# Four fewer filler matmuls, an earlier key mask, and a product kept in PSUM, in a four-layer image kernel

## The reference

```python
x = x + window_attention(_gn(x))      # 7 x 7 windows, shifted by 3, 8 heads of 8 channels, softmax
x = x + _L1_conv_ref(_gn(x))          # signs of x (*) signs of the kernel, times Ka, plus bias
x = x + _L2_conv_ref(_gn(x))          # 3 x 3 convolution with the sign of its kernel
x = x + _L3_conv_ref(_gn(x))          # expand, 4-tap convolution along the tokens, silu gates, contract
```

```python
beta = mean(|xp|, channels)                                   # xp: x padded by 1
K = reduce_window(beta, add, 3 x 3) / 9
Ka = K * mean(|kernel|, (0, 1, 2))
return conv(sign(xp), sign(kernel)) * Ka + bias
```

## Time and profile before

| what | value |
|---|---|
| median of 3 runs | 222.25 us |
| the runs | 222.25, 220.94, 222.32 us |
| the profiled execution's own time | 222.39 us |
| its span, first to last instruction | 220.5 us |
| its mean granted TensorE clock | 0.992 |

### The profile page before, as it was taken

How to read it: one execution, slowest core, us unless ns; L and a number is a source line. 1 busy time by engine, 2 the same in 40 slices (tenths; PEclk the granted TensorE clock), 3 DMA queues, 4 the chain that set the end, 5 groups by cost and what they waited for, 6 DMA issues and landing times.

```text
span 220.5 us, 6793 instructions
## 1 busy us (share of the span) xinstructions
PE 206.8 (94%) x2734; PEld 144.1 (65%) x2735; DVE 158.5 (72%) x316; ACT 138.9 (63%) x294; POOL 95.4 (43%) x108
## 2 busy tenths in 40 slices
PE   7888999999999999999999999689799999899994
PEld 2456788888878778888787765444456665445441
DVE  4665699976978778868789739699997763616533
ACT  2438697778886898769877452168345363966631
POOL 0349999871124397241970158187324311000000
PEclk9999999999999999999999999799999999999999
DMA  6960000000000000000000000000165710001023
GB/s 210 443 263 0 3 3 6 0 4 3 3 3 3 3 4 0 3 3 4 3 3 0 4 3 0 3 20 22 42 135 126 178 23 0 0 3 73 0 106 113
DMA packets 4701, 10.03 MB, mean 45 GB/s; under 512 B 704, under 2 KB 3520, under 8 KB 4544
## 3 DMA queue, kind: packets, MB, share of 16 engines
q1 hardware_dynamic: 4528, 9.27, 13.3%
q10 hardware_dynamic: 144, 0.34, 0.4%
HBM read 5.03 MB, written 1.61 MB: 30 GB/s over the span
## 4 chain that ended last, share of the span: by engine, by line
PE 73%; DVE 12%; ACT 6%; issue 4%; DMA 2%; POOL 1%; SPq 1%; ACTq 0%; DVEq 0%; POOLq 0%
PE turned L707 12%; PE outs L727 10%; PE scores L696 10%; PE scores L915 5%; PE scores L916 4%; PE qkv L667 4%; PE qkv L677 4%; PE turned L943 3%; PE scores L824 3%; DVE x L1156 3%; PE scores L637 2%; PE outs L749 2%; DMA p<-parts 2%; PE scores L933 2%; PE turned L860 2%
## 5 line engine op out<-in xcount | busy, mean ns | idle before, releaser
L1036 DVE TENSOR_REDUCE mx<-scores 113x16 f32<-113x784 f32 x32 | 30.9, 965 | 9.5 <-PE scores L696 9.3
L707 PE MATMUL turned<-cst,d 113*113 113x113 f32 x256 | 33.3, 273 | 0.9 <-DVE d L1041 0.9
L707 PEld LDWEIGHTS turned<-cst,d 113*113 113x113 f32 x256 | 27.8, 178 | 8.5 <-issue 7.1
L476 ACT ACTIVATE pt<-turned 113x392 f32<-113x392 f32 x64 | 28.4, 495 | 7.1 <-PE turned L707 5.8
L1041 DVE TENSOR_TENSOR d<-scores,mx 113x784 f32<-113x784 f32 x32 | 31.2, 976 | 1.1
L208 POOL TENSOR_TENSOR kex<-ks,cst 128x784 f32<-128x784 f32 (+1 forms) x16 | 23.2, 1451 | 18.7 <-ACT ks L455 18.5
L288 POOL TENSOR_TENSOR rstd<-ve,mhalf 128x1 f32<-128x1 f32 (+1 forms) x15 | 8.7, 578 | 51.8 <-DVE ve L1002 51.7
L727 PEld LDWEIGHTS outs<-vsb,pt 113*49 113x49 f32 x1024 | 26.1, 125 | 6.1 <-issue 2.9
L446 ACT ACTIVATE scores<-rel 113x784 f32<-113x784 f32 x32 | 26.2, 818 | 5.0 <-PE scores L637 3.9
L727 PE MATMUL outs<-vsb,pt 113*49 113x18 f32 x1024 | 29.2, 199 | 0.0
L696 PE MATMUL scores<-kex,qs 32*49 32x196 f32 x512 | 28.2, 332 | 0.0
(11 more groups left out here) (121 smaller groups left out, 370.7 us busy)
## 6 DMA issues: line engine op xcount, KB each, us to landing
p<-parts SPq DMA_DIRECT2D x20, 112.5 KB, 2.2
x<-x_in SPq DMA_DIRECT2D x1, 1568.0 KB, 9.8
out<-res SPq DMA_DIRECT2D x8, 196.0 KB, 1.9
xw<-xw_in SPq DMA_DIRECT2D x2, 392.0 KB, 4.8
xw<-xw_in SPq DMA_DIRECT2D x1, 784.0 KB, 6.7
p<-parts SPq DMA_DIRECT2D x6, 108.8 KB, 3.0
ker<-ker_in SPq DMA_DIRECT2D x2, 288.0 KB, 10.1
late<-late_in SPq DMA_DIRECT2D x1, 417.0 KB, 10.7
```

Of the source, the lines that this page charges most:

```text
L476: act.activation(pt[0:WK, k % 2, j].rearrange("p n (w t) -> p n w t", w=2), ps_t[j][0:WK, :].rearrange("p (n w t) -> p n w t", n=4, w=2)[: ...
L707: mm = pe.transpose(ps_t[j][0:WK, n * P:n * P + WK], d[0:WK, k % 2, h:h + 2, :].rearrange("p a b -> p (a b)")[:, 0:WK], ident[0:WK, 0:WK])
L1036: dve.tensor_reduce(top, sc, AXX, ALU.max).then_inc(max_done, 1)
```

## The change

Three edits. The four fillers are taken out between `proj_v(0)` and `scores(0)` (2 stay of 6). On DVE, the mask of windows 0 and 1 now stands ahead of the moments of group 1. In `finish1` the product is written back into the PSUM bank that it was read from, and the second instruction reads it there; the SBUF tensor `prod` is gone.

```diff
-        prod = sb("prod", [P, 2, HALF])
@@ PE
             proj_v(0)
-            filler(ps_t[1], 6)
+            filler(ps_t[1], 2)
             pe.wait_ge(init_dve, 2)
             scores(0)
@@ DVE, start
+            dve.wait_ge(ks_ready, 1)
+            mask_keys(dve, 0, 0, 2).then_inc(kex_first, 1)
             dve.wait_ge(ld_x1, 16)
             window_moments(1).then_inc(gn_stats, 1)
-            dve.wait_ge(ks_ready, 1)
-            mask_keys(dve, 0, 0, 2).then_inc(kex_first, 1)
@@ DVE, finish1
-                dve.tensor_tensor(prod[:, i], bk[u % 4][:, 0:HALF], ka[:, i], ALU.mult).then_inc(prod_done, 1)
+                ps = bk[u % 4][:, 0:HALF]
+                dve.tensor_tensor(ps, ps, ka[:, i], ALU.mult).then_inc(prod_done, 1)
                 dve.wait_ge(prod_done, u + 1)
-                dve.scalar_tensor_tensor(out=xx, in0=prod[:, i], scalar=ww("b1"), in1=xx, op0=ALU.add,
+                dve.scalar_tensor_tensor(out=xx, in0=ps, scalar=ww("b1"), in1=xx, op0=ALU.add,
                                          op1=ALU.add).then_inc(x_done, 1)
```

## The result

The changed kernel took 219.4 us (median of 4 runs: 217.16, 218.76, 220.04, 220.09), the kernel before 221.79 us beside it (220.94 to 222.32, 4 runs): ratio 0.9898, 95% interval 0.9852 to 0.9945. That is faster by 1.0%, inside the forecast range and 1.5 us above the forecast 217.9.

What follows compares the result with a forecast made beforehand. PE was taken as the bound, with 73% of the chain that ended last. Span 220.5 - 0.93 - 0 - 2.1 - 1.3 = 216.2; with 1.9 outside the span, less 0.14, 217.9 us; range 216.4 to 220.5.

Steps and rivals of the forecast that it cites:

- Part 1: At the start, four of PE's six fillers ahead of the first scores go: gain 0.93 us.
- for PE both are early enough: At the start, whichever of DVE and POOL masks first, DVE's mask (near 11.4 or 12.23) does not hold PE.
- Part 2: At the start, DVE's mask moves ahead of the moments: costs 0 to 0.08 us, taken as 0.
- the cover to the hundredth: At the start, two fillers would end at 12.29, just behind DVE's mask at 12.23 in the old order.
- Part 3: In the first convolution, the product in PSUM frees L1156 from waiting for POOL: 2.1 us, bounds 0.87 and 4.2.
- The slot between the two box sums: In the first convolution, `third_part(dve, 0)` gets in between POOL's L331 and L333, with some 0.6 us to spare.
- Part 4: At PE's gap ahead of `mix` (138 to 140 us), a shorter wait avoids the half clock behind it: 1.3 us.
- rival 1: The half clock stays or turns up elsewhere: 219.2 us; chance 0.25 with the clock's part of rival 5.
- rival 5: Less PE work before 13 us drops the clock near 15 us, costing some 1.3 us; chance counted within rival 1's 0.25.
- rival 2: In the convolution, a missed slot or late ACT copies wait the gain away: 220.4, or 219.1 with the clock's; chance 0.12.
- rival 3: In `finish1`, L1156 is long for another reason and stays 1.36 us, only the fillers count: 221.3 us; chance 0.08.
- rival 4: In `finish1`, DVE reads and writes one PSUM bank in turns, 0.41 us more per product: 223.6 us; chance 0.05.

Runs made afterwards that it cites:

- the kernel with the mask last: The changed kernel without its two fillers ahead of the first scores, DVE's mask back behind the moments: 218.42 us, ratio 0.9873 to the kernel before.

## Why the prediction was right, and where it failed

The forecast was 217.9 us and the result 219.4: right in its sign and its range, with a fall of 2.4 us where 4.3 were forecast. Step by step:

- **Part 1** said 0.93 us. Measured alone 0.74 in the trace, 0.81 in the time at full clock. The step that failed is "for PE both are early enough" (said in part 2) and the cover to the hundredth: I compared ends with starts, and left out that the scores start a quarter of a microsecond after the mask's end (12.00 and 12.25 here, 11.85 and 12.11 in the kernel with the mask last). With the mask first the stretch is 0.53 us instead of 1.40, which is 0.87.
- **Part 2** said that the move alone gains nothing measurable. True beside six fillers (0.02 us). With two it gives 0.13 us (0.66 to 0.53), and with none 0.6. DVE did come first, by 0.1 us.
- **Part 3** said 2.1 us up to POOL's `third_part(1)`, of which 0.87 in group 0 and 1.23 behind it. Measured there, at full clock: 2.10, with 0.86 and 1.24. That is not luck, since the steps between hold one by one in the full-clock traces: 1.30 us are gained by `remainder(0)`, two `nmr` give 0.2 each, the box sum at L333 costs 0.4, and the `mix` gives 0.75 (0.7 forecast). The slot between the two box sums was found as described: 1.36 us for the third part (about 1.4 forecast). The path behind `third_part(1)` was taken as dense, and it was not. From there to the end of the span it is 60.6 to 61.0 us in the three full-clock traces with groups 1 to 3 in SBUF, and 59.7 to 60.4 in the seven with them in PSUM; by the times it is 0.5 us, 2.58 in all. The product's surcharge for writing PSUM, bounded by 0 and 0.41, is 0.006 us. Of the Trainium skill's 62 cycles more for a PSUM source ("VectorE: DVE Perf Modes", section "The TRN2 errata — SBUF-src ops pay a fixed extra latency per instruction"), the trace shows nothing: the addition takes 626 ns with a PSUM source and 627 undisturbed with an SBUF one.

  The chain that ended last in the fillers-only kernel (start, duration, what), ahead of `conv2(3)`:

```profile
170.90 0.60 SPq L262
171.54 0.60 SPq L262
172.19 1.79 SPq L262
174.02 2.30 DMA p<-parts
176.46 0.70 PE scores L838 x6
```

  SP's queue issues its DMAs back to back there, and PE waits for the last (0.27 us idle). With the product in PSUM these transfers start earlier, and the chain of the changed kernel's undisturbed run has no DMA behind `conv2(1)`. That this is all of the 0.5 us isn't shown: the kernel with no fillers and the mask first has the product in PSUM and such a wait too (0.30 us).

- **Part 4 is the step that failed.** It said that the half clock goes with the gap, for 1.3 us. The first half of it is shown: filling that gap alone brought 12 of 12 runs to full clock, and with group 0 in PSUM, which leaves 0.97 us of its 1.82, 11 of 12. But rival 1 came true as well. It spoke of a new wait of PE for box sums of about 1.7 us; the trace of before had this wait already, 1.51 us long, and the change made it 2.12. The clock fell behind it in two traces, and with it filled six of six runs stayed up. The change swapped one place for another. The early half clock of the profiled run, worth 1.7 us, was not foreseen: rival 5 looked for a fall near 15 us, this one came at 7 us, ahead of the edit in PE's list.
- The size in part 4 was off too. It took the 1.3 us between 220.94 and 222.25 for the price of the half clock, but 220.94 lies above all 24 full-clock runs, of which the slowest took 220.87. From 222.25 to full clock it is 1.8 us. So the base was the slower level, and the changed kernel's full-clock runs, at 217.33, lie below the forecast.
- At full clock the changed kernel takes 217.33 us against 220.44, 3.1 us less, and the sum without the clock was 3.0. That these agree so well is in part luck: the start gave 0.06 less than forecast and the end more, and the parts measured alone add up to 3.4 (0.81 + 2.58), or 3.5 with the mask's 0.13. The 0.3 to 0.4 us between the parts and the whole are not explained. In the traces they lie behind `third_part(1)`, where the changed kernel's undisturbed run waits 0.40 us for a DMA ahead of `conv2(1)` and the product-only run doesn't wait.
- What of the 219.4 is the change? Its ten runs have a median of 218.38, the kernel before 221.2 in most groups. The four first runs held both of the doubly disturbed ones. With the mean clock known for each run the two effects can be told apart; with medians of four they can't.
- **Rivals 2, 3 and 4** fall: the slot was not missed, L1156 lost its delay to the nanosecond, and the product in PSUM costs 6 ns. Rival 5, a clock fall by the removal of fillers, has no support: 4 of 12 at full clock without them, 24 of 68 with them.

## What to carry to other kernels

Follow a change along the waits to a named point, and check it there in a run at the same clock: that sum held to a hundredth, while the kernel's time moved by 3 us for another reason. When VectorE reads two SBUF tensors beside GpSimd, look at the spread of one line's durations; moving one input to PSUM removed it here. And when a chain beside PE gets faster, look for the waits of PE that it makes longer, not only for the one that it mends, since the clock may fall there as it did in the old one. Filler matmuls into a free bank, ended before the wait does, delayed `third_part(1)` by 0.03 us in the traces of both kernels that had them.

## What was unexpected of the hardware

- DVE read and wrote the same PSUM bank in one instruction at full rate: 566 ns for 392 columns, against 560 into SBUF.
- A half-clock stretch cost 1.8 us in some runs of the kernel before and 0.7 in others (medians 222.25 and 221.1 against 220.44), and both vanished with the gap. No kept trace is of a run near 221.1, so why there are two levels is open.
- Five of six runs kept the clock with both waits at their longest (groups 1 to 3 in PSUM, 1.84 and 2.12 us), and five of six with the later one alone (no fillers at the start), where the changed kernel kept it in 3 of 10. Whether that is chance in six runs or the moment at which the gap comes was not tried.
